# Moving the rounding of h to GpSimd, one step later, in the FP4 feed-forward stage of a retention + FFN kernel

## The reference

```
x = layernorm(x + retention(x))
gate = fp4_linear(x, w_gate);  up = fp4_linear(x, w_up)       # 256 -> 704 each
h = silu(gate) * up
x = layernorm(x + fp4_linear(h, w_down))                       # 704 -> 256

def fp4_quant_dequant(x):          # in blocks of 16 along the last axis
    scale = max(max(abs(xb)) / 6, 1e-12)
    xn = xb / scale
    q = nearest of {0, .5, 1, 1.5, 2, 3, 4, 6} to |xn|, with xn's sign, times scale
```

## Time and profile before

| | |
|---|---|
| median of 3 runs | 579.48 us |
| the profiled execution's own time | 580.2 us |
| its span (first to last instruction) | 578.3 us |
| busy: PE, PEld | 561.6 us (97%), 485.5 us (84%) |
| busy: DVE | 512.8 us (89%), 1279 instructions |
| busy: ACT | 337.3 us (58%) |
| busy: POOL | 228.6 us (40%), 260 instructions |
| granted PE clock, mean | 0.997 |
| chain that ended last | PE 83%, DVE 7%, issue 4%, POOL 2% |

### The profile page before, as it was taken

How to read it: one execution, slowest core, us unless ns; L and a number is a source line. 1 busy time by engine, 2 the same in 40 slices (tenths; PEclk the granted TensorE clock), 3 DMA queues, 4 the chain that set the end, 5 groups by cost and what they waited for, 6 DMA issues and landing times.

```text
span 578.3 us, 14061 instructions
## 1 busy us (share of the span) xinstructions
PE 561.6 (97%) x4440; PEld 485.5 (84%) x4440; DVE 512.8 (89%) x1279; ACT 337.3 (58%) x818; POOL 228.6 (40%) x260
## 2 busy tenths in 40 slices
PE   7999999999999999999999999999999999999994
PEld 3778888888888888888888788889999999999983
DVE  6667878999999999899999889999999999888886
ACT  4445766777686677768667754534454555445442
POOL 2211121534334343442534214565654655654420
PEclk9999999999999999999999999999999999999998
DMA  7711210110111011011101000000010100000002
GB/s 206 227 26 41 56 47 12 56 54 1 54 54 36 18 54 51 4 54 54 33 22 36 20 18 2 1 0 2 1 38 1 38 15 25 18 20 19 19 19 92
DMA packets 24983, 22.32 MB, mean 39 GB/s; under 512 B 2025, under 2 KB 21874, under 8 KB 24946
## 3 DMA queue, kind: packets, MB, share of 16 engines
q1 hardware_dynamic: 24130, 20.27, 11.5%
q10 hardware_dynamic: 816, 1.57, 0.9%
HBM read 17.63 MB, written 4.20 MB: 38 GB/s over the span
## 4 chain that ended last, share of the span: by engine, by line
PE 83%; DVE 7%; issue 4%; POOL 2%; DMA 2%; ACT 1%; ACTq 0%; DVEq 0%; POOLq 0%
PE wide_banks L1371 46%; PE wide_banks L1587 10%; PE wide_banks L1442 9%; PE wide_banks L1419 4%; PE wide_banks L1430 3%; PE wide_banks L1559 3%; PE turn L1468 3%; PE turn L1405 2%; PE wide_banks L1455 2%; DVE shared L862 1%; DMA pow_dram<-powers 1%; POOL shared L1332 1%; PE turn L1568 1%; DVE shared L867 1%; DVE shared L684 1%
## 5 line engine op out<-in xcount | busy, mean ns | idle before, releaser
L1337 POOL TENSOR_TENSOR shared<-shared,h_scale 128x704 f32<-128x704 bf16 x31 | 43.1, 1392 | 78.3 <-DVE shared L867 76.0
L1371 PE MATMUL wide_banks<-win_hi,x_hi 128*128 128x512 f32 x192 | 65.5, 423 | 3.4 <-DVE win_lo L945 1.6
L1442 PEld LDWEIGHTS wide_banks<-shared 128*128 128x128 f32 x512 | 62.0, 192 | 2.8
L469 ACT ACTIVATE shared<-opened,rstd 128x64 f32<-128x64 f32 x240 | 63.5, 339 | 1.0
L566 ACT ACTIVATE shared<-wide_banks 128x512 f32<-128x512 f32 x64 | 29.6, 463 | 53.6 <-PE wide_banks L1371 53.1
L1442 PE MATMUL wide_banks<-shared 128*128 128x64 f32 x512 | 60.6, 271 | 0.0
L1371 PE MATMUL wide_banks<-win_hi,x_lo 128*128 128x512 f32 x192 | 60.4, 396 | 0.0
L1371 PE MATMUL wide_banks<-win_lo,x_hi 128*128 128x512 f32 x192 | 60.3, 395 | 0.0
L1371 PE MATMUL wide_banks<-wgu_hi,xq_hi 128*128 128x512 f32 (+1 forms) x192 | 59.7, 392 | 0.6 <-DVE xq_lo L1078 0.6
L435 ACT ACTIVATE shared<-shared 128x704 bf16<-128x704 f32 x32 | 25.3, 791 | 54.7 <-POOL shared L1332 52.3
L1371 PE MATMUL wide_banks<-wgu_lo,xq_hi 128*128 128x512 f32 (+1 forms) x192 | 56.5, 375 | 0.0
(11 more groups left out here) (150 smaller groups left out, 1442.8 us busy)
## 6 DMA issues: line engine op xcount, KB each, us to landing
xf<-in_x_feat SPq DMA_DIRECT2D x32, 128.0 KB, 2.3
tab<-in_tables SPq DMA_DIRECT2D x16, 256.0 KB, 2.8
xt<-in_x_tok SPq DMA_DIRECT2D x32, 128.0 KB, 2.1
out<-x SPq DMA_DIRECT2D x32, 128.0 KB, 1.7
x<-in_w_in ACTq DMA_DIRECT2D x3, 512.0 KB, 5.8
w<-in_w_gu SPq DMA_DIRECT2D x1, 1408.0 KB, 8.6
w<-in_w_down SPq DMA_DIRECT2D x1, 704.0 KB, 9.9
wgu_lo<-pow_dram SPq DMA_DIRECT2D x1, 576.0 KB, 4.8
```

Of the source, the lines that this page charges most:

```text
L469: last = act.activation(gated[:, b, cols], opened[:, b, cols], ACT.Copy, scale=rstd[:, b, 1 + k:2 + k])
L1337: pool.tensor_tensor(over_blocks(hq[:, b]), over_blocks(h_steps[:, b]), spread(h_fp4["scale"][:, b]), ALU.mult).then_inc(h_fp4["ready"], 1)
L1371: last = pe.matmul(dst, lhs, rhs, start=k == 0, stop=k == len(parts) - 1)
L1442: last = pe.matmul(mixed[:, r, DV * at:DV * (at + 1)], ret[:, slot(k)], vs[:, b, DV * k:DV * (k + 1)], start=False, stop=k >= HEADS - 2, s ...
```

## The change

- **h's rounding.** `h_round` leaves DVE and becomes two operations on POOL: a TENSOR_SCALAR max(size, 1.5 * 2^22) in place (128x704, bf16) and a TENSOR_TENSOR subtraction (128x704), each waiting for the one ahead by a semaphore. POOL does them for tile n-2 in step n, and `rescale_h` for tile n-2 behind them, where before it was tile n-1. `rescale_x` moves ahead of `h_to_unit`. The last tile's rounding stays on DVE.
- **The late x's roundings.** `round_up` and `round_down` for x tiles 27 to 31 (eight passes in steps 4, 5, 10, 11, 16, 17, 22, 23) leave POOL for DVE, ahead of `h_shift`.
- **Down product.** The 64 repeated rows of h's last high chunk take the low half of rows 640 to 703, and the same rows of the high weights take a copy of the high weights of these rows. The hi*hi product so includes lo*hi of the last chunk, and the third sum has 5 matmuls, not 6. `split_h` on DVE becomes one operation of 128x640 and one of 64x128; one memset goes, and ACT makes one more small copy.
- **Norms.** The root's chain goes over 8 tiles at a time (`EIGHT`), so once in eight steps; the outputs of a group of eight follow two tiles per step.

```diff
             def h_round(n, b):                                   # now in POOL's program
+                need(pool, h_fp4["ready"], n - 1)
+                pool.wait_ge(h_shifted, n + 1)
+                pool.tensor_scalar(h_size[:, b], h_size[:, b], SIZE_FROM, None, ALU.max).then_inc(h_floored, 1)
+                pool.wait_ge(h_floored, n + 1)
+                pool.tensor_tensor(h_steps[:, b], h_size[:, b], h_unit[:, b], ALU.subtract).then_inc(h_fp4["rounded"], 1)
...
             def ffn_body(n, k):                                  # POOL
                 b = k % 2
+                if valid(n + 2):
+                    rescale_x(n + 2, b)
                 if valid(n - 1) and n < TILES:
                     h_to_unit(n - 1, 1 - b)
-                if valid(n + 2):
-                    rescale_x(n + 2, b)
-                if n in (4, 10, 16, 22):
-                    round_up({4: TILES - 2, 10: TILES, 16: TILES + 2, 22: TILES + 4}[n])
-                elif n in (5, 11, 17, 23):
-                    round_down({5: TILES - 2, 11: TILES, 17: TILES + 2, 23: TILES + 4}[n])
-                if valid(n - 1) and n < TILES:
-                    rescale_h(n - 1, 1 - b)
+                if valid(n - 2) and n <= TILES:
+                    h_round(n - 2, b)
+                    rescale_h(n - 2, b)
...
             def ffn_body(n, k):                                  # DVE
...
-                if quant:
+                if n == TILES:
+                    dve.wait_ge(h_fp4["rounded"], n - 1)
                     h_round(n - 1, 1 - b)
-                if n == TILES:
                     rescale_h(n - 1, 1 - b)
...
             def late_x(n, b):                                    # DVE
...
+                elif n in (4, 10, 16, 22):
+                    round_up({4: TILES - 2, 10: TILES, 16: TILES + 2, 22: TILES + 4}[n])
+                elif n in (5, 11, 17, 23):
+                    round_down({5: TILES - 2, 11: TILES, 17: TILES + 2, 23: TILES + 4}[n])
...
             def split_h(n, b):                                   # DVE
-                dve.tensor_tensor(hT_lo[:, b], turned_h, hT_hi[:, b].bitcast(F32), ALU.subtract).then_inc(hT_lo_ready, 1)
+                dve.tensor_tensor(hT_lo[:, b, 0:FULL], turned_h[:, 0:FULL], hT_hi[:, b, 0:FULL].bitcast(F32), ALU.subtract)
+                dve.tensor_tensor(hT_hi[0:F_OLD, b, FULL:FC * P], turned_h[F_OLD:P, FULL:FC * P],
+                                  hT_hi[F_OLD:P, b, FULL:FC * P].bitcast(F32), ALU.subtract).then_inc(hT_lo_ready, 1)
...
             def down(n, b):                                      # PE
-                parts = [(t[:, b, P * c:P * (c + 1)], w[:, c]) for t, w in
-                         ((hT_hi, wdown_hi), (hT_hi, wdown_lo), (hT_lo, wdown_hi)) for c in range(FC)]
+                parts = [(t[:, b, P * c:P * (c + 1)], w[:, c]) for t, w, chunks in
+                         ((hT_hi, wdown_hi, FC), (hT_hi, wdown_lo, FC), (hT_lo, wdown_hi, FC - 1)) for c in range(chunks)]
```

More of the change, by code:

```diff
@@ L47 @@
 F_OLD = FC * P - FF
+FULL = (FC - 1) * P
 EPS = 1e-5
@@ L77 @@
 QUAD_STEPS = 12
+EIGHT = 2 * QUAD
 def slot(h):
@@ L334, in width, with chain_of @@
             return DM * len(tiles_of(n))
+        def chain_of(n):
+            first = n - n % QUAD - EIGHT - QUAD
+            if n - n % QUAD == QUAD:
+                return 0, range(QUAD - LAG, QUAD), None
+            if first >= 0 and first % EIGHT == 0 and n < TILES:
+                return 1 + first // EIGHT, range(EIGHT), first
+            return None
         def loads(n, b):
@@ L553, in turn_weights @@
                 if old < BANK:
-                    act.activation(wdown_hi[F_OLD:P, c + 1], src[F_OLD:P, old:BANK], ACT.Copy).then_inc(w_hi_ready, 1)
+                    for rows in (slice(0, F_OLD), slice(F_OLD, P)):
+                        act.activation(wdown_hi[rows, c + 1], src[F_OLD:P, old:BANK], ACT.Copy).then_inc(w_hi_ready, 1)
             def split_xq(n, b):
@@ L972, in turn_weights @@
                     dve.tensor_tensor(wdown_lo[F_OLD:P, c + 1], src[F_OLD:P, old:BANK], wdown_hi[F_OLD:P, c + 1].bitcast(F32), ALU.subtract)
-                    for part in (wdown_hi, wdown_lo):
-                        last = dve.memset(part[0:F_OLD, c + 1].bitcast(F32), 0.0)
+                    last = dve.memset(wdown_lo[0:F_OLD, c + 1].bitcast(F32), 0.0)
                 last.then_inc(w_lo_ready, 1)
@@ L1050, in quad_root @@
                 dve.wait_ge(quad_step, done + 11)
-                if first > 0:
+                if first:
                     dve.wait_ge(out_ready, first)
@@ L1095, in ffn_body @@
                 out, quant = valid(n - 5), valid(n - 1)
-                first = n - 2 * QUAD - k
-                chain = first >= -QUAD and n < TILES
-                slots = range(QUAD) if first >= 0 else range(QUAD - LAG, QUAD)
-                done = QUAD_STEPS // QUAD * (first + QUAD)
+                chain = chain_of(n) is not None
+                if n >= TILES:
+                    number, slots, first = 4, range(QUAD), TILES - EIGHT
+                elif chain:
+                    number, slots, first = chain_of(n)
+                if chain or n >= TILES:
+                    done = QUAD_STEPS * number
                 if n > TILES:
@@ L1107, in ffn_body @@
                 if out:
[L1108 removed]
+                    out_stats(n - 5, (n - 5) % EIGHT)
                 if quant:
@@ L1112, in ffn_body @@
                     if k == 0:
-                        quad_moments(n - 5 if first >= 0 else -1, slots)
+                        quad_moments(-1 if first is None else n - 5, slots)
                     elif k == 1:
@@ L1152, in ffn_body, with round_up, round_down @@
                         quad_poly(done, slots)
-                if quant:
+                if n == TILES:
+                    dve.wait_ge(h_fp4["rounded"], n - 1)
                     h_round(n - 1, 1 - b)
-                if n == TILES:
                     rescale_h(n - 1, 1 - b)
+            def round_up(n):
+                unit, rounder = (x_fp4[k][:, 0, 0:width(n)] for k in ("unit", "rounder"))
+                dve.wait_ge(x_fp4["rounder_ready"], n - 2)
+                dve.tensor_tensor(unit, unit, rounder, ALU.add).then_inc(x_fp4["rounded"], 2)
+            def round_down(n):
+                unit, rounder = (x_fp4[k][:, 0, 0:width(n)] for k in ("unit", "rounder"))
+                dve.wait_ge(x_fp4["rounded"], n - 2)
+                dve.tensor_tensor(columns(steps_flat, n), unit, rounder, ALU.subtract).then_inc(x_fp4["ready"], 2)
             def late_x(n, b):
```

59 lines of the change are left out of this document (30 added, 29 removed).

## The result

The changed kernel took 629.92 us (median of 5 runs, 628.03 to 632.53) beside 579.53 for the one before: a ratio of 1.0867, 95% interval 1.0846 to 1.0887. The profiled execution is the longest of the five, 632.53 us at a mean granted clock of 0.975; the two with 0.994 and 0.995 took 628.03 and 628.38. Its span is 630.3 us against 578.3, 52.0 more.

What follows compares the result with a forecast made beforehand. PE was taken to bound the kernel, DVE close behind; after the change, POOL and DVE's ring. 580.2 + 18.8 + 8 - 1.7 + 1.5 + 2.7 = 609.5, less 0.7: 609 us, range 585 to 631.

Steps and rivals of the forecast that it cites:

- the gap: POOL's idle time ahead of h_to_unit, while DVE does scales and reciprocal: 0.67 us a step.
- rival 3: POOL's max is a dear operation, 1.71 us or above: 8.24 us a step, 630 us in all; chance 0.14.
- the forecast's own case: Main stretch: POOL and DVE make steps of 7.1 to 7.9 us, 597 to 623 us in all; chance 0.58.
- 28 steps: Steps 3 to 31 of the main stretch, each going from 6.81 to 7.48 us: +18.8 us.
- the sum's term of +2.7: A term of +2.7 us in the forecast's sum; its derivation is not in the text given.
- the ring: POOL's five operations and DVE's waiting on each other in a loop: 6.06 + 0.67 + 0.75 = 7.48 us a step.
- The max, a: POOL's added TENSOR_SCALAR max in h's rounding: 0.95 us taken, bounds 0.70 and 1.71.
- The subtraction, b: POOL's added subtraction in h's rounding, with two full inputs: 1.71 us taken, lower bound 1.39.
- The hold: DVE's h_shift waits for a POOL operation's end, then keeps POOL's next one back: 0.75 us a step.
- Late x, +8: Late-x passes on DVE, with the moments of eight tiles ahead of the reciprocal: +8 us, bounds 0 and 14.
- Start, end: Start: two roundings ahead of step 3's h_to_unit go, -1.7 us. End: later last products and more splits, +1.5 us.
- Rival 1: Faster or unchanged kernel, outside the range: chance 0.09 with a gain, 0.05 with the reload eating it.

Runs made afterwards that it cites:

- e3: Changed kernel with three buffers for h's scales, so h_scale of tile t waits for rescale_h of tile t-3 only: 627.58 us.
- e12: Changed kernel with POOL's max done on only the first 352 of 704 columns: 617.74 us.
- e7: Changed kernel with h_shift of tiles 4 to 30 reading a PSUM column in place of h_unit in SBUF: 620.44 us.
- e11: Changed kernel with the eight late-x rounding passes on DVE narrowed to 16 columns each: 627.94 us.
- e5: Changed kernel with POOL's max replaced by a TENSOR_TENSOR that adds a zero: 626.96 us.
- e6: Changed kernel with the eight late-x rounding passes back on POOL, behind h_to_unit: 634.39 us.
- e1: Changed kernel with h's rounding, rescale_h's tile and the late-x passes put back as in the kernel before: 579.98 us beside 579.87.
- e10: Changed kernel with h_shift of tiles 4 to 30 reading a PSUM column, plus 6 unused PE matmuls ahead of turn_h's wait: 618.73 us.
- e9: Changed kernel with 8 more unused PE matmuls ahead of turn_h's wait in each step from 4 on: 629.39 us.
- e8: Changed kernel with h's rounding back as in the kernel before, only the late-x passes staying moved to DVE: 577.84 us beside 579.88.

## Why the prediction was right, and where its sizes were off

The direction held, and in the quiet steps the mechanism: PE waits for rescale_h, POOL is 85% busy with its five operations end to end, the gap is 0.68, and where h_shift is held it ends 0.75 us after a POOL operation. But 609 was forecast and 629.92 came. The stated range of 585 to 631 took it in by 1 us, and only because its upper end was put there for rival 3; given the forecast's own case the range was 597 to 623, and the time lies outside it. That part is luck.

By the profiled executions the miss is 632.5 - 609.5 = 23.0 us: the 28 steps cost 50.5 and not 18.8 + 8 (+23.7), the start and the end 1.7 more, and the sum's term of +2.7 isn't in the trace. In 11 of the 28 steps POOL isn't full, and the ring is longer for something that the prediction doesn't name. Opening the ring's closing wait gave 2.3 us only (e3): the single ring explains the quiet steps and not the others. The ring of 7.48, term by term against the quiet step of 8.21:

- **The max, a.** Taken at 0.95 with an upper bound of 1.71; it is 1.965, +1.02 a step, the largest error. The bound rested on "one input is at most as dear as two". e12 gives 2.49 ns a column against the 2.17 that the earlier trace rows gave for two float32 inputs. Rival 3 (a at 1.71 or above, 630) named the right time and the right cause for the larger part, though its ring of 8.24 meets 8.21 by errors that cancel: a is 0.25 short in it, the hold 0.28 too long.
- **The subtraction, b.** 1.71 taken, 1.53 to 1.54 measured: with one bf16 input and a bf16 output it is cheaper than the float32 line, -0.17.
- **Between the operations.** POOL waits for its own semaphores: the subtraction starts 0.08 after the max's end, rescale_h 0.15 after the subtraction's, where operations without such a wait overlap by 0.03 to 0.05. Net +0.16, not counted. So 1.39 + 1.97 + 1.54 + 1.38 + 0.62 + 0.68 + 0.16 = 7.74, which e7 shows.
- **The hold.** POOL's half of it was a choice, borne weakly by the earlier trace rows. It is real (2.02 at 555.41, 1.85 at 411.56), and e7 removes it with its cause. Its size in a quiet step is 0.47, not 0.75: h_shift starts in the max, which doesn't hold it (0.88 us at 555.13), and only its rest falls into the subtraction. In eight of the 28 steps it is h_shift that is held, up to 2.24 us.
- **28 steps.** By the quiet step, 28 x (8.21 - 6.81) = 39.2 us instead of 18.8.
- **Late x, +8.** What the steps last beyond 8.21 is 28 x 0.40 = 11.2 us, part of it the low clock of this execution, and it isn't mainly the eight passes (e11). Three edits of POOL's work moved the time by half of it or less: e5 3.0 of 17, e12 12 of 25, e6 4.5 of 9.3. There is a second path, which the prediction left out: it checked DVE only from h_shift's end on, and took h_shift's start for given. From rescale_h's end, PE's turn_h (0.87) and gate_up (2.45), then DVE's product for h (L1101, 0.89), h_shift (0.88), the addition of the down product, maxima and statistics (1.72), scales and inverse (some 0.8), with hand-overs some 7.8 us, lead to the h_to_unit that POOL reaches after one whole step and 1.30 more, at 8.21 + 1.30 = 9.5. Its 1.7 us of slack are used up by a held h_shift (+1.35), a slow turn_h, or operations of DVE that are held. From 498.47 + 1.38 to 510.91 it took 11.06. The path is worked out from rows; no run took it away by itself. e3's steps of 7.0 and 9.4 in turn, and the idle time that grew in e5 and e12, fit it.
- **Start, end, the term of +2.7.** Step 3's h_to_unit is at 360.90, 1.5 us earlier (forecast 1.7). The end, from step 31 on, is 28.3 us against 25.3, +3.0 (forecast +1.5). No run shows the sum's term of +2.7, the reload that the chances name. What the trace has at L1369 ahead of the first max are two MODIFY_POOL_CONFIG of 11 ns each, at 354.0, and the max of 354.07 follows within 0.05 us of h_to_unit's end.

Part of what DVE does on that path is small. A piece of the norm's root, before and then after, by form:

```profile
L1031 DVE SCALAR_TENSOR_TENSOR fine<-rsq,root 128x4 f32<-128x4 f32 x8 | 1.2, 155 | 0.1
```

```profile
L1046 DVE SCALAR_TENSOR_TENSOR fine<-rsq,root 128x8 f32<-128x8 f32 x3 | 3.4, 1144 | 0.0
```

An operation of 0.155 us takes 1.14 on average where it meets a POOL operation. The width isn't the cause: in e1, also at 128x8, it takes 0.162. The hold is paid per instruction: this one took up to 1.51 us, h_shift up to 2.24, each 1.35 more than when free. So the norms over eight tiles, which cost nothing in e1, do stand in long steps together with the moved roundings (e10). How the 11 us divide among these, the late x's passes and PE's lateness stays open: e9, e10 (against e7) and e11 each took something away and got 0.5, 1.7 and 2.0 us.

Rival 1, which has the chances of "faster" and "same", is out: the time is 8.7% up and the quiet step 8.21. Of the 2.9 us that the prediction counted for 17 matmuls, e8 shows 2.0, and there POOL does nothing while any h_shift runs.
